# 24 dense and 16 gathered tiles a step in 41 steps, counts written to columns read from a table, codes' one-hots without gaps

## What is computed

```
h   = relu(layernorm(x));  deg = max(count of dst, 1)
msg = (h[src] + relu(attr @ W1e + b1e) @ W2e + b2e) * (deg[src] * deg[dst]) ** -0.5
agg = segment_sum(msg, dst)
c   = (1 + eps) * h + agg;  o = relu(c @ W1n + b1n) @ W2n + b2n + h
out = x + o * rsqrt(mean(o * o) + 1.2e-7) * rms_w
```

## Time and profile before

| what | value |
|---|---|
| median of 3 runs (range) | 1078.37 us (1076.29 to 1084.59) |
| the profiled execution's own time | 1070.17 us |
| its span, first to last instruction | 1068.3 us |
| busy: PE, DVE, POOL, ACT | 956.5, 914.1, 746.8, 651.4 us |
| granted clock over the span | 0.993 |

### The profile page before, as it was taken

One profiled execution on the slowest core, in us unless ns is written; L12 is line 12 of the kernel. 1 busy time (PEld: TensorE's weight loads), 2 busy tenths in 40 slices (PEclk: granted clock), 3 DMA queues, 4 the chain that ended last, 5 costly groups with the idle time before them and its releaser, 6 DMA issues. The chain is left out here.

```text
span 1068.3 us, 35619 instructions
## 1 busy us (share of the span) xinstructions
PE 956.5 (90%) x12753; PEld 765.3 (72%) x12753; DVE 914.1 (86%) x4066; ACT 651.4 (61%) x1747; POOL 746.8 (70%) x754
## 2 busy tenths in 40 slices
PE   0333999999999999999999999999999999999985
PEld 0332787887887887777887887787777788788753
DVE  6998988988988988988988988987887898898668
ACT  7972666666665665666666666666566666566435
POOL 2035777777777777777777777777777777777374
PEclk9999999999999999999999999999999999999988
DMA  6035455455554454455454455454455545452473
GB/s 240 15 147 202 145 150 141 139 153 143 142 156 143 138 161 143 133 163 144 123 173 140 129 172 136 131 163 130 141 147 150 143 140 157 141 135 67 157 299 106
DMA packets 57740, 156.99 MB, mean 147 GB/s; under 512 B 16051, under 2 KB 23398, under 8 KB 57184
## 3 DMA queue, kind: packets, MB, share of 16 engines
q1 hardware_dynamic: 33776, 104.43, 29.1%
q0 software_dynamic: 22784, 47.07, 18.8%
q10 hardware_dynamic: 1008, 3.21, 0.9%
HBM read 147.95 MB, written 6.70 MB: 145 GB/s over the span
## 5 line engine op out<-in xcount | busy, mean ns | idle before, releaser
L1065 POOL DMA_INDIRECT arena<-node_rows,idx x712 | 702.3, 986 | 228.9 <-issue 153.3
L1236 ACT ACTIVATE arena<-bank 128x294 f16<-128x294 f32 x900 | 327.2, 420 | 256.2 <-PE bank L1141 239.3
L1226 ACT ACTIVATE arena<-bank 128x512 f32<-128x512 f32 x405 | 222.6, 596 | 105.9 <-PE bank L1091 99.6
L1151 PE MATMUL bank<-t_words,arena 128*128 128x256 f16 x2205 | 276.2, 272 | 0.4 <-DVE arena L1354 0.4
L1291 DVE TENSOR_SCALAR arena<-iota_c,code 128x294 f16<-128x294 f16 x900 | 273.7, 359 | 2.3 <-PE bank L1141 2.3
L1304 DVE SCALAR_TENSOR_TENSOR arena<-iota_h,hi_f,bank 128x49 f32<-128x49 f32 x900 | 184.0, 260 | 77.6 <-PE bank L1106 75.7
L1141 PE MATMUL bank<-arena 128*128 128x294 f16 x900 | 206.2, 307 | 18.8 <-DVE arena L1291 12.4
L1091 PEld LDWEIGHTS bank<-w1e,arena 64*128 64x128 f32 x3240 | 215.6, 190 | 4.7
L1091 PE MATMUL bank<-w1e,arena 64*128 64x128 f32 x3240 | 218.1, 272 | 0.0
L1151 PEld LDWEIGHTS bank<-t_words,arena 128*128 128x128 f16 x2205 | 199.0, 97 | 21.2 <-issue 0.6
L1141 PEld LDWEIGHTS bank<-arena 128*128 128x128 f16 x900 | 101.4, 144 | 83.2 <-issue 37.1
(11 more groups left out here) (210 smaller groups left out, 804.9 us busy)
## 6 DMA issues: line engine op xcount, KB each, us to landing
arena<-in_attr SPq DMA_DIRECT2D x90, 512.0 KB
arena<-low_src SPq DMA_DIRECT2D x47, 652.5 KB, 7.6
arena<-node_rows,idx POOLq DMA_INDIRECT x712
arena<-in_attr SPq DMA_DIRECT2D x45, 128.0 KB
node_rows<-arena SPq DMA_DIRECT2D x1, 3160.5 KB, 8.9
arena<-in_x ACTq DMA_DIRECT2D x7, 448.0 KB, 10.9
arena<-in_x SPq DMA_DIRECT2D x6, 512.0 KB, 12.6
out<-arena SPq DMA_DIRECT2D x12, 224.0 KB
```

The source lines that it names most:

```text
L1065: nc.gpsimd.indirect_dma_start(out=edge_rows[:, u, j, 0:ROW], out_offset=None, in_=table, in_offset=bass.IndirectOffsetOnAxis(ap=idx[:, c, ...
L1151: mm = nc.tensor.matmul(x_sum[:, 0:2 * D], strip[:, u, k, :], T16[:, k, :], start=k == 0, stop=k == NBLK - 1)
L1226: nc.scalar.activation(out.rearrange("p (j o) d -> p o j d", o=2), z[:, :, j0:j0 + n // 2, :], ACT.Relu).then_inc(r_ready, 1)
L1236: nc.scalar.activation(strip[:, u, :, tile * W:tile * W + W], pair_bank[:, j * 512:j * 512 + CW].rearrange("p (k w) -> p k w", w=W), ACT.C ...
```

## The change

It deals the work anew: TD = 24 and TG = 16, so 41 steps of 40 tiles, 984 dense and 628 gathered tiles (900 and 712 before). The fifth phase now has two units too. Pairs are counted in the order of `FIRST_PAIR` and `MORE_PAIRS`; phases 2 and 3 have three pairs each, one of them in the middle of the phase's spread share. `look` takes 2, 2, 2, 3 and 3 pairs. The windows have 112 and 88 columns for 96 and 96.

24 tiles of 6 columns don't fit in the 128 columns of `strip`. So a tile now takes as many columns as it has targets: the prologue computes each tile's first column (`column_at`), ACT loads it into a register and copies its 6 columns there, and the next tile of the same half overwrites what is too much. That asks for an order of the copies (`strip_ready` in `keep_counts`). What the old fixed places gave for free, the place of each strip column in the window, is computed in the prologue too (new operations on POOL, four PE matmuls, and DVE). `edge_rows` keeps the gathered rows double but the relu's output single. `code_oh` has no gap any more between its groups of 6 (`WS` 6 for 8). ACT copies the counts of `FIRST_PAIR[p]` between the two relus of a phase. The diff, cut to its core:

```diff
-WIN = 96
-TD, TG = 20, 16
+WD, WG = 112, 88
+TD, TG = 24, 16
 TS = TD + TG
-LOOKS = [0, 2, 4, 6, 8, 10]
-UNITS_D = [(0, 4), (4, 4), (8, 4), (12, 4), (16, 4)]
+LOOKS = [0, 2, 4, 6, 9, 12]
+UNITS_D = [(0, 4), (4, 4), (8, 4), (12, 4), (16, 4), (20, 4)]
 UNITS_G = [(0, 4), (4, 4), (8, 4), (12, 4)]
 UD, UG = len(UNITS_D), len(UNITS_G)
 U = UD + UG
-PHASES = [(0, 1), (2, 3), (4, 5), (6, 7), (8,)]
+PHASES = [(0, 1), (2, 3), (4, 5), (6, 7), (8, 9)]
 NPH = len(PHASES)
-SPREAD_AT = [0, 10, 12, 27, 42, 49]
+SPREAD_AT = [0, 10, 14, 31, 48, 49]
+FIRST_PAIR = [1, 3, 5, 8, 11]
+MORE_PAIRS = [(2,), (4,), (6, 7), (9, 10), ()]
 UL = TD // 2
 RL = 2
 PB = 3
-GROUP_AT = [0, 5, 10, 15]
+GROUP_AT = [0, 6, 12, 18]
...
-ATTR_PAIRS = [0, 8, 16, 18]
+ATTR_PAIRS = [0, 8, 16, 20]
...
-WS = 8
-XC = TD * W
+WS = W
 XS = 128
-NPASS = -(-N // W)
+WSAFE = W - 1
+NPASS = -(-N // WSAFE)
 NA = TD // 2
-LB = 10
+LB = 6
...
-        loop.edge_rows = take(2, TG, XW).rearrange("p (u t w) -> p u t w", u=2, t=TG)
+        loop.edge_rows = take(TG, 2 * ROW + D + 1).rearrange("p (t w) -> p t w", t=TG)
...
+            sp.dma_start(slots[:, :, :].rearrange("p a t -> p (a t)").bitcast(I32), t["slots"]).then_inc(slots_in, 16)
             sp.dma_start(heads.bitcast(I32), t["heads"].broadcast_to((128, S * TS))).then_inc(heads_in, 16)
+            sp.dma_start(tails.bitcast(I32), t["tails"].broadcast_to((128, S * TS))).then_inc(tails_in, 16)
             sp.dma_start(head_off.bitcast(I32), t["head_off"]).then_inc(edge_in, 16)
...
+            pool.wait_ge(consts, 11)
+            pool.wait_ge(slots_real, 1)
...
+            step(nc.gpsimd.tensor_tensor(in_rows(widths[:, 0, :]), tails_s, heads_s, ALU.subtract))
+            step(nc.gpsimd.tensor_scalar(widths[:, 0, :], widths[:, 0, :], float(W - 1), 1.0, ALU.min, ALU.add))
+            step(nc.gpsimd.memset(widths[:, 0, NA - 1:NA], float(W)))
+            a = 0
+            for by in (1, 2, 4, 8, 16):
+                nc.gpsimd.tensor_copy(widths[:, 1 - a, 0:by], widths[:, a, 0:by])
+                step(nc.gpsimd.tensor_tensor(widths[:, 1 - a, by:TD], widths[:, a, by:TD], widths[:, a, 0:TD - by], ALU.add))
...
+            pool.sem_inc(starts_ready, 1)
+            step(nc.gpsimd.tensor_tensor(beyond_safe[:, :], starts[:, :], safe_starts[:, :], ALU.subtract))
+            pool.wait_ge(fast_ready, 1)
+            step(nc.gpsimd.tensor_tensor(starts[:, :], beyond_safe[:, :], fast[0:S, 0:1].broadcast_to((S, TD + 1)), ALU.mult))
+            nc.gpsimd.tensor_tensor(head_at[:, :], head_at[:, :], fast[0:S, 0:1].broadcast_to((S, TD)), ALU.mult)
+            step(nc.gpsimd.tensor_tensor(starts[:, :], starts[:, :], safe_starts[:, :], ALU.add))
+            nc.gpsimd.tensor_copy(column_at[:, :], starts[:, :])
+            step(nc.gpsimd.tensor_tensor(head_at[:, :], head_at[:, :], starts[:, 0:TD], ALU.subtract))
+            step(nc.gpsimd.tensor_tensor(jumps[:, 0:TD - 1], head_at[:, 1:TD], head_at[:, 0:TD - 1], ALU.subtract))
+            own_step = ident[0:S, 0:S].unsqueeze(2).broadcast_to((S, S, TD))
+            for a, of in ((0, starts[:, 1:TD + 1]), (1, jumps[:, :])):
+                nc.gpsimd.tensor_tensor(spread_out[:, a, :, :], own_step, of.unsqueeze(1).broadcast_to((S, S, TD)), ALU.mult).then_inc(columns_ready, 1)
...
+                    pool.wait_ge(deg_done, 1)
+                    pool.wait_ge(split_in, 16 * 12)
+                    nc.gpsimd.memset(strip_words, 0.0).then_inc(strip_clear, 1)
...
+            pe.wait_ge(columns_ready, 2)
+            for a in range(2):
+                numbers_of = spread_out[:, a, :, :].rearrange("p s t -> p (s t)")
+                for n0 in range(0, S * TD, 512):
+                    n1 = min(S * TD, n0 + 512)
+                    mm = nc.tensor.matmul(bank2[a][:, n0:n1], ones[0:S, :], numbers_of[:, n0:n1], start=True, stop=True)
+            mm.then_inc(columns_turned, 1)
...
+            nc.vector.tensor_scalar(off[:, 1:3, :], off[:, 1:3, :], fast[:, 0:1], win_pos[:, 0:1], ALU.mult, ALU.add)
+            v.wait_ge(columns_turned, 1)
+            passed = code[:, :, :].rearrange("p s t -> p (s t)")
+            step(nc.vector.tensor_scalar(passed, bank2[0][:, 0:S * TD], part_f[:, 0:1], None, ALU.is_le))
+            step(nc.vector.tensor_tensor(passed, passed, bank2[1][:, 0:S * TD], ALU.mult))
+            step(nc.vector.tensor_reduce(off[:, 0, :], code[:, :, :], AX.X, ALU.add))
+            nc.vector.tensor_scalar(off[:, 0, :], off[:, 0, :], part_f[:, 0:1], None, ALU.add)
...
-                                pool.wait_ge(tile_ps, 2 * (after + 6))
+                                pool.wait_ge(tile_ps, 2 * (after + 7))
                             else:
-                                pool.wait_ge(strip_ready, 2 * (after + 5))
+                                pool.wait_ge(strip_ready, 2 * (after + 6))
                         nc.gpsimd.indirect_dma_start(
-                            out=edge_rows[:, u, j, 0:ROW], out_offset=None, in_=table,
+                            out=edge_rows[:, j, row_at(u):row_at(u) + ROW], out_offset=None, in_=table,
...
-                nc.tensor.matmul(turned_bank[:, 0:WIN], sum_d, place[:, 1, :], start=True, stop=True)
-                nc.tensor.matmul(turned_bank[:, WIN:2 * WIN], sum_g[:, D:2 * D], place[:, 2, :], start=True,
+                nc.tensor.matmul(turned_bank[:, 0:WD], sum_d, place[:, 1, :], start=True, stop=True)
+                nc.tensor.matmul(turned_bank[:, WD:WD + WG], sum_g[:, r_at(c):r_at(c) + D], place[:, 2, 0:WG], start=True,
                                  stop=True).then_inc(turned_ps, 1)
...
-                        count_pair(c, u, 2 * p + 1)
+                        count_pair(c, u, FIRST_PAIR[p])
                     if live(c + 1):
                         look(c + 1, p)
+                    more = MORE_PAIRS[p] if live(c) else ()
                     if c == S and p == 0:
                         spread_rows(c - 1, 1 - u, 0, NBLK)
-                    elif c < S and live(c - 1) and SPREAD_AT[p] < SPREAD_AT[p + 1]:
-                        spread_rows(c - 1, 1 - u, SPREAD_AT[p], SPREAD_AT[p + 1])
+                    elif c < S and live(c - 1):
+                        k0, k1 = SPREAD_AT[p], SPREAD_AT[p + 1]
+                        half = (k0 + k1) // 2 if len(more) > 1 else k1
+                        spread_rows(c - 1, 1 - u, k0, half)
+                        if len(more) > 1:
+                            count_pair(c, u, more[0])
+                            spread_rows(c - 1, 1 - u, half, k1)
+                    elif len(more) > 1:
+                        count_pair(c, u, more[0])
                     if live(c - 2) and p == 0:
                         window_gathered(c - 2)
                         window_dense(c - 2)
                     if live(c - 1) and last:
                         turn(c - 1)
-                    if live(c) and not last:
-                        count_pair(c, u, 2 * p + 2)
+                    if more:
+                        count_pair(c, u, more[-1])
...
-                    if not (isinstance(c, int) and c < 2):
-                        act.wait_ge(summed_g, (c - 2) * UG + (k - UD + 1))
-                    out = edge_rows[:, u, first:first + n, ROW:XW]
+                    if not (isinstance(c, int) and c < 1):
+                        act.wait_ge(summed_g, (c - 1) * UG + (k - UD + 1))
+                    out = edge_rows[:, first:first + n, ROW:ROW + D]
...
+            def load_columns(c, pairs):
+                for j in range(2):
+                    at = j * NA + pairs[0]
+                    _, values = nc.values_load_multi_w_load_instructions(
+                        column_at[c:c + 1, at:at + len(pairs)], engines=(act.engine,), min_val=0, max_val=XS - W,
+                        skip_runtime_bounds_check_because="the prologue takes these columns only where the last one is at most XS - W")
+                    for p, value in zip(pairs, values):
+                        column_of[2 * p + j] = value
             def keep_counts(c, u, p):
                 for j in range(2):
                     act.wait_ge(tile_ps, 2 * (c * NA + p) + (j + 1))
+                    if p > 0:
+                        act.wait_ge(strip_ready, 2 * (c * NA + p - 1) + (j + 1))
                     if p == 0 and j == 0 and not (isinstance(c, int) and c < 2):
                         act.wait_ge(x_ps, c - 1)
-                    tile = 2 * p + j
-                    nc.scalar.activation(strip[:, u, :, tile * W:tile * W + W],
+                    nc.scalar.activation(strip[:, u, :, bass.ds(column_of[2 * p + j], W)],
...
-                        if p > 0:
-                            keep_counts(c, u, 2 * p)
-                        relu(c, u, 2 * p)
-                        if p < NPH - 1:
-                            relu(c, u, 2 * p + 1)
-                        keep_counts(c, u, 2 * p + 1)
+                        for q in MORE_PAIRS[p - 1] if p > 0 else ():
```

(17 more changed lines are left out.)

220 lines of the change are left out of this document (135 added, 85 removed).

## The result

The changed kernel takes **1120.0 us** (median of 4, 1118.79 to 1120.12), the kernel before 1078.23; the ratio is 1.0367 (95% interval 1.033 to 1.0404). I had forecast 1082 with 1055 to 1106. It is slower, and by more than the range allowed.

What follows compares the result with a forecast made beforehand. PE was taken to pace the edge pass. 1068.3 − 80.5 (four fewer steps) − 3.9 (late gathers) + 84.0 (longer steps) + 8.5 (prologue) = 1076.4; 1.9 more gives 1078.3, and half of 8.2 gives 1082 us, range 1055 to 1106.

Steps and rivals of the forecast that it cites:

- Bound: Edge pass: PE paces the step, with POOL almost as tight before the change; DVE is not the bound.
- POOL's relief: Gathers on POOL: 16 need 20.1 of 22.2 us, 2 to spare, so the 3.9 us of late gathers go.
- PE's own work, 21.30 a step: PE in an edge step: 20.13 less 0.57 of old stalls plus 1.74 of added work, 21.30 us.
- The new order, T + 1.79: Relu B behind two copies: next edge_mlp starts 1.79 us after the count's start T; PE waits 0.49 (phase 1), 0.29 (phase 4).
- phase 0 0.30 for 0.15: Spread in phase 0 waits for keep_x behind DVE's last picks: +0.15 us a step, between 0 and 0.5.
- Register loads: ... so 0.92 fits: 0.: Two loads a phase ahead of relu A, 0.46 us each on ACT, fit in its slack: 0 added.
- the limit of 1.1: ACT has about 1.1 us between its last copy and relu A; loads and their wait beyond that decide rival 2.
- Rival 2: Loads ahead of relu A can't start before the previous copy ends: step 0.5 us longer, 1102 us; chance 0.16.
- The copies' cost, left at 0.41: ACT's copies of counts at the new columns: old timing kept, the second copy adding 0.31 us.
- Prologue, +8.5 (4 to 13): Before the steps, paid once: later POOL masks, wider DVE operations, longer tables and DMAs add 8.5 us, bounds 4 and 13.
- so 40 and not 41: First step has no spread and no keep_x, so the 2.10 us a step counts 40 times, 84.0 us.
- From the profile to the median: The earlier kernel's median stands 8.2 us above its profile; half of that was added, giving 1082 us.

Runs made afterwards that it cites:

- e1: Changed kernel without the register loads, every copy of counts going to a fixed, even column: 1076.71 us, ratio 0.9966 to the kernel before.
- e4: Changed kernel with both relus of a phase ahead of the copies of FIRST_PAIR again: 1159.12 us, ratio 1.0721 to the kernel before.
- e3: Changed kernel without the register loads, every copy of counts going to fixed, odd columns (8k + 1 and 8k + 3): 1118.1 us, ratio 1.0348 to the kernel before.
- f3: Changed kernel, load of slots issued behind that of heads, strip's clear behind the last mask: 1407.36 us on a chip where the kernel before takes 1354.47.
- e12: Changed kernel, prologue only: POOL masks before placing columns, tails load behind src_d, strip's clear behind last mask: 1406.31 us, chip where kernel before takes 1354 to 1356.

## Why the prediction was wrong

- **Bound.** PE's own work is 21.05 of the 22.96 us of a step and still paces the pass; right. But of the 1.90 left all except the 0.16 of phase 0 are waits for ACT, 0.78 in the forecast. POOL's relief came as said: it has 325 us of idle time.
- **PE's own work, 21.30 a step:** 21.05 measured. Each count pair takes 0.29 for 0.31, and the other terms hold within 0.06. Right.
- **The new order, T + 1.79:** waits at the places and of the sizes said (e1: 0.44 and 0.25 for 0.49 and 0.29; phase 0 0.30 for 0.15). Right. What the sum did not see is that the order is what lets the third pair be counted at all in time (e4).
- **"Register loads: ... so 0.92 fits: 0."** This step failed. I took 0.46 for a load, from a row that loads one number. A load takes 0.29 and 0.21 for each number more, 0.73 for the three of phases 2 and 3, so two take 1.5 and not 0.92; the limit of 1.1 that I had named myself is passed. Rival 2 named the place and the sign, but not the reason: its condition, that a load can't start before the copy ahead of it has ended, is not what the rows show (517.7 against 518.23). Of its price of 0.5 a step, 0.35 at least is shown (e3).
- **The copies' cost, left at 0.41.** This step failed without being written down: the sum copied the old duration to new places in memory. Columns 1, 3 and 7 modulo 8 cost 0.2 us. e1 and e3 give the upper end, 0.94 a step if all are long; what 35% of them cost was not measured by itself. The sum for both is 0.67 in phases 2 and 3, 0.15 in phase 1 and 0.14 in phase 4 above my figures, and phases 2 and 3 are free of waits in e1. 918.5 against 40 × 22.23 = 889.2 is 29 us of the miss, the larger part of it.
- **Prologue, +8.5 (4 to 13).** +16.06 to the first `look`, above the bound: +10.42 up to `rel_d`, −1.35 from there to L691 (L609 before), +6.99 behind that. The POOL chain was well sized: L634 waits 4.85 for it, against 4.5. Missing were `heads` 6.1 us later (converted at 15.97 for 9.86), which only the small load beside it explains, and the clear of `strip`, which holds L691 for 2.9 us. That these two stood in the chain is read from the rows; when f3 and e12 took one or both away, other waits gave back all but 0.1 and 1.1 us. The parts, rows of DVE and POOL of the changed kernel, answering:

```profile
15.97 1.02 DVE L527 CAST t_words<-t_words 128x1640 f32<-128x1640 int32 x1 [1.82 <-DMA t_words<-in_heads]
...
38.68 1.18 DVE L634 TENSOR_SCALAR rel_d<-t_words 128x984 f32<-128x984 f32 x1 [4.85 <-POOL t_words L432]
...
76.01 3.98 DVE L691 TENSOR_SCALAR t_words<-t_words,fast 128x1640 f32<-128x1640 f32 x1
```

```profile
73.76 5.36 POOL L439 MEMSET arena<- 128x6272 f32 x1 [2.61 <-DVE stat L682]
```

- **The first step** costs 4.55 more than before, and the sum gave it nothing but the longer tables ("so 40 and not 41"). Its added work went missing with that: in e1, without loads and odd columns, it is 1.73 more than before (31.99 for 30.26), close to the 1.74 by which the sum raised every other step. Some 1.6 are the clock, which the sum did not foresee: the granted clock is 1.00 from 107 to 131.8 us, with PE busy for 16.2 of these 24.8, and then 0.57 over the next 4, so for most of them at its lower level, 1.2 for 2.4 GHz. L1201 takes 1.40 there for 1.05, and L1229 2.78 for 1.52 in later steps. Neither e1 (PE busy for 17.1 of the same 24.8) nor the kernel before has such a stretch there. The last 1.2 or so are left for loads and odd columns. PE's waits for the copies are not what is new: it waits five times before, 3.9 us in all, and six times after, 3.5 us. The stretch of 4 us (busy us of PE, PEld, DVE, ACT and POOL; the granted clock is the third number from the end), and PE's rows in it:

```profile
131.80:135.80 4.00, 4.00 (x64) 3.23 (x63) 0.37 (x1) 0.83 (x2) 2.73 (x3) 0.57 0.62 132
```

```profile
131.52 1.40 PE L1201 MATMUL bank<-w1e,arena 64*128 64x128 f32 x16
132.85 2.78 PE L1229 MATMUL bank<-arena 128*32 128x128 f32 x48
```

- **From the profile to the median.** I added half of the 8.2 us by which the median of the kernel before stands above its own profile. The changed kernel's profiled execution takes 1120.03, which is its median, so this term is 0. It moved the forecast 4 us towards the measured time by luck; the sum by itself said 1078.3.
- **The port.** "Shows no gather lengthened" was a wrong reading of the trace of before: I had looked at one gather. Its gathers (ns min/median/max) are mostly at 0.94, but 0.986 in the mean and up to 1.70:

```profile
L1065 POOL DMA_INDIRECT arena<-node_rows,idx x712: 940/944/1700, 75.0 to 1000.6; - x178
```

  Those at 82.55 to 88.54 last 1.68 to 1.70 each, for as long as DVE runs L648:

```profile
86.53 1.70 POOL L1065 DMA_INDIRECT arena<-node_rows,idx  x1 [0.30 <-issue]
```

```profile
82.33 7.09 DVE L648 TENSOR_TENSOR t_words<-arena,t_words 128x896 f16<-128x896 f32 x7
```

  So gathers do lose time to DVE, which the sum had put at 0, but little: the mean went from 986 to 1010 ns, and POOL has room. DVE loses where POOL's operation is long: L691 ended 0.87 after the clear, about its own length of 1.07. The Trainium skill, page "SBUF — State Buffer", section on who interferes with whom, says just that of a fast-mode operation; the trace agrees, and e12 shows it a second time on L702 and L703.
- **The Trainium skill**, page "Runtime: NRT & Kernel Launch", section on instruction fetch mechanics, gives about 200 ns for each register of a load, there for loads from HBM. The rows agree for loads from the chip's own memory, with 0.21 for each number more. By that figure, as an estimate, a load of three is 0.6 and two are 1.2, just above the limit of 1.1, so rival 2 deserved more than its 0.16.

Even with both misses of the step away, e1 stands at 1077 and the kernel before at 1078: 40 tiles in 21.94 are 0.549 us a tile, 36 in 20.13 are 0.559, and the longer prologue and first step take the rest. No version that computes the whole result beat the kernel before.

## What to carry to other kernels

When a change makes an address dynamic, price three things apart: the load of each register (by the number loaded, not by the instruction), the engine's wait at the place where the loads stand, and the operation's own duration at the new offsets; a duration read at aligned, fixed places doesn't carry over. And before moving the operation that a chain waits for, look for what is late next: three edits to the prologue gave back 1 us of 10.
